# Small matmuls set one by one between long passes: scores, values and transposes of an attention and feed-forward kernel

## The chip, the cores and the metric

The kernel runs on one core of a Trainium2 chip. What is measured is the device time of one execution in microseconds (us). TensorE does the matmuls, ScalarE the tables and copies, VectorE elementwise work and sums, GpSimd (POOL) more elementwise work, and SyncE (SP) issues transfers.

## The reference

Two branches share one layer norm of `x` (4 batches of 1024 tokens, 512 wide), and both are added to it:

```python
xn = _layernorm(x)
x = x + attn(xn) + ffn(xn)
# attn: 8 heads, q and k of 32 per head, v of 64
h_in = _rmsnorm(x, norm1_w)
q, k, v = h_in @ wq, h_in @ wk, h_in @ wv          # by head
o_pre = h_in @ w_og
i_pre = soft_cap(h_in @ w_ig + b_ig); f_pre = soft_cap(h_in @ w_fg + b_fg)
Fcum = cumsum(log_sigmoid(f_pre))
Dmat = where(causal, Fcum[s] - Fcum[t] + i_pre[t], -inf); m = max(Dmat)
C = (q @ k.T / sqrt(32)) * exp(Dmat - m)
h = (C / maximum(abs(sum(C)), exp(-m))) @ v
h_out = sigmoid(o_pre) * rmsnorm_per_head(h)
x1 = x + h_out @ w_out
h2 = _rmsnorm(x1, norm2_w)
attn = x1 + silu(h2 @ w_gate) * (h2 @ w_up) @ w_down     # 2048 wide
# ffn: the same form, 1376 wide, its weights read from a table of 16 by indices
ffn = silu(x @ Wg.T) * (x @ Wu.T) @ Wd.T,  W = lut[idx]
```

## The kernel before, in words

**Blocks.** The work goes in eight blocks of 512 tokens, two per batch. Large matmuls work on operands split in a high and a low part and make three passes of 512 columns for each 128 of the inner dimension (high with high, low with high, high with low; `split`, L797): 12 passes for 512. A block of the attention branch has a **front** (`front`, L1073: gates, twelve projections `proj(n)`, L813, of 12 passes each, 0 to 3 for q and k, 4 to 7 for v, 8 to 11 for the output gate) and eight **units** (one per chunk of 128 tokens and group of four heads). A unit u is three pieces on TensorE: `unit_1` (four score matmuls, L879), `unit_2` (one matmul `kv`, L888, and four of the values, L891, each fp32 and so two instructions in the trace), `unit_3` (state, L899). Between them the other engines make exponentials, products and head sums.

**Tiles.** The feed-forward part of a block has 16 **tiles**, each `gate` and `up` (12 passes each) and `down` of the tile before (8 passes with `hidden_hi`, L1021, then 4 with `hidden_lo`, L1024). The tiles of one block run beside the units of the next: `tiles` (L1101) holds a table `fill` of what stands after `gate`, after `up` and after `down` of tile t. In tiles 0 to 7 these are `unit_1(t)`, `unit_2(t)` and `unit_3(t)`; then come `out_proj`, in tile 10 the transposes `h2_T` (L932), in tile 15, ahead of `down`, the sixteen transposes `x_T` (L943) of the next block's normed input, four banks of four. After the tiles follow `gates` of the next block (L1038), which needs `x_T` split in high and low parts by ScalarE (L1199) and VectorE (L1673), and the last `down`. In the front the transposes `q_k_T(i)` of q and k (L849) stand between whole projections, four for each chunk i of 128 tokens, all in the one bank `gate_bank`; ScalarE copies it twice (L1385, L1386) and VectorE subtracts for the low part (L1844). `gate_rows` (L1058) and `factors` (L1066) are small transposes for the gates.

**The first block.** It has no block before it, so its eight units run beside the projections of the second: for each u, `unit_1(u+1)`, nine passes of `proj(u-1)`, `unit_2(u)`, the last three passes, `unit_3(u)`. Then come `proj(6)`, `gate_rows`, `proj(7)`, `ho_T(3)` (transposes of the attention output, L844), `proj(8)`, four `out_proj`, `h2_T` with `proj(9)` and `proj(10)` between and after, `factors`, `proj(11)`, and the tiles.

**The end.** After the last attention block its 16 tiles run alone, and then the second branch: eight blocks of 11 tiles, with nothing between them. Its weights are decoded by `look` steps, beside the attention work, on ScalarE (L1274 to L1304) and VectorE.

**Order.** Every engine runs a program written out by hand, in order; the engines wait for each other by counters. Loads are issued by SP in its own written order. On ScalarE a tile is, among others, `hid(t-1)` (makes `hidden_hi`, L1212), the tanh of `gate` (L1207), exponentials, `h2_T` evacuations at t = 10, and the look-up steps; the low part of the hidden values comes from POOL (L2195). VectorE's order in the first block has `gate_factors` (L1820) between `x1_(0)` and `x1_(1)` (L1735), POOL's the four `x1_root` and `mlp_lo_` (L2180).

Of the kernel before, what the change touches and what calls it, by code (L numbers as in the profile page):

```python
# [5 lines left out]
P = 128  # L6
D = 512
KT = D // P
H = 8
DQ = 32  # L10
DV = 64
VS = DV + 1
# [138 lines left out]
def program(nc, x, w_attn, w_gates, norm1, b_gates, mh_w, norm2, w_mlp, lut, idx, out):  # L151
# [3 lines left out]
    with ctx:  # L155
# [636 lines left out]
        def _(pe):  # L792
# [11 lines left out]

            def pair(t, *ix):
                return (t[0][ix], t[1][ix])
# [6 lines left out]
            def proj(at, n, begin=0, end=3 * KT):  # L813
# [35 lines left out]
            def q_k_T(at, i):  # L849
                wait(pe, act_qk, at, i, "k")  # L850
                if i:
                    wait(pe, act_qkT, at, i - 1, "done")
                    if not here(at, FIRST):
                        wait(pe, vec_qkT, at, i - 1, "lo")
                else:
                    tiles_left(pe, MLP.gated, at)
                transposes(GB, [qn(at, i)[:, g * P:(g + 1) * P] for g in range(G)]
                           + [kn_(at)[:, i, g * P:(g + 1) * P] for g in range(G)], pe_qkT)

            def unit_1(at, u):  # L860
# [17 lines left out]
                for h in range(HG):  # L878
                    mm = pe.matmul(B[:, toks(h)], stack[0:3 * DQ, u % 2, 1, toks(h)], stack[0:3 * DQ, u % 2, 0, toks(h)],  # L879
                                   start=True, stop=True)  # L880
                mm.then_inc(pe_unit.sem, 1)

            def unit_2(at, u):
# [5 lines left out]
                for h in range(HG):  # L889
                    c = (j * H + g * HG + h) * VS  # L890
                    mm = pe.matmul(pick(at, u, A, ACC[0])[:, h * P:h * P + VS], pick(at, u, ct, ct2)[:, h, :], va_(at)[:, c:c + VS], start=True, stop=True)  # L891
                mm.then_inc(pe_unit.sem, 1)
# [39 lines left out]
            def h2_T(at, i):  # L932
                wait(pe, vec_h2, at, i)
                if here(at, FIRST):
                    wait(pe, vec_x1, at, i, "x1")
                elif i < 2:
                    wait(pe, vec_x1, at, i + 2, "x1")
                else:
                    wait(pe, vec_h2S, at, i - 2, "scaled")
# [3 lines left out]
            def x_T(at, i, src):  # L943
# [10 lines left out]
                elif here(at, FIRST):  # L954
                    if i >= 2:
                        wait(pe, vec_xT, at, i - 2, "lo")
# [1403 lines left out]
```

## Time and profile before

| | |
|---|---|
| median of 3 runs | 2401.63 us (2400.05 to 2402.75) |
| the profiled execution | 2400.62 us |
| its span in the trace | 2398.8 us |
| mean granted TensorE clock | 0.998 |
| TensorE busy | 2364.2 us, 99%, 11424 instructions |
| VectorE, ScalarE, POOL busy | 50%, 37%, 27% |

The span runs from the first instruction to the last in the trace; the execution's own time is 1.8 us longer. Busy time of TensorE counts a pass as it lies in the pipeline, so 99% says that something is nearly always in it, not that it runs at its peak. One row of the timeline is a group of like instructions: start, duration from the first start to the last end, engine, line, operation, output and inputs, count, and in brackets the idle time before it with what ended it.

### The profile page before, as it was taken

The page shows a single profiled execution, that of the slowest core. Times are in us where ns is not written, and L with a number is a line of the kernel's source. Part 1 is how long each engine was busy: PE and PEld are TensorE (multiplying, and loading weights), DVE is VectorE, ACT ScalarE, POOL GpSimd, SP SyncE. Part 2 cuts the span into 40 slices and gives each one's busy share as a digit, 9 for nine tenths or more (in the row PEclk, how much of TensorE's full clock was granted, in tenths as well). Part 3 has the DMA queues.
Part 4 walks back from the last instruction along what each step waited for, and adds up shares of the span by engine and source line. Part 5 has one row for each costly group of instructions (what it writes and reads, how often), then busy time and mean ns, then how long its engine had stood idle before and what let it go on. Part 6 is the DMA issues. An engine that isn't in the chain of part 4 may idle for free. (4 is left out here: it accounts for less than half of the span.)

```text
span 2398.8 us, 30880 instructions
## 1 busy us (share of the span) xinstructions
PE 2364.2 (99%) x11424; PEld 1937.2 (81%) x11424; DVE 1197.9 (50%) x2133; ACT 899.1 (37%) x1653; POOL 636.4 (27%) x494
## 2 busy tenths in 40 slices
PE   8899999999999999999999999999999999999999
PEld 6677888888888888888888888888888888888887
DVE  6776536665674674567467466642222222222222
ACT  6533244444445454445545453562111111111111
POOL 2356513223331321322232232322111111111111
PEclk9999999999999999999999999999999999999999
DMA  6277576576567558657755764766876876876865
GB/s 241 77 246 254 225 284 213 197 280 221 180 238 260 190 206 291 198 186 249 245 194 207 276 214 171 274 239 213 301 255 239 298 250 241 300 251 238 302 217 208
DMA packets 184035, 561.76 MB, mean 234 GB/s; under 512 B 17968, under 2 KB 75568, under 8 KB 148688
## 3 DMA queue, kind: packets, MB, share of 16 engines
q1 hardware_dynamic: 158400, 518.50, 61.9%
q10 hardware_dynamic: 25488, 41.30, 5.2%
q8 instruction: 92, 1.51, 0.3%
q14 instruction: 55, 0.45, 0.1%
HBM read 456.18 MB, written 102.50 MB: 233 GB/s over the span
## 5 line engine op out<-in xcount | busy, mean ns | idle before, releaser
L801 PE MATMUL gate_bank<-act_hi,gud 128*128 128x512 f32 x1728 | 573.5, 393 | 0.5 <-DVE th L1724 0.5
L801 PE MATMUL up_bank<-act_hi,gud 128*128 128x512 f32 x1728 | 572.8, 393 | 0.0
L2195 POOL TENSOR_TENSOR hidden_lo<-hm,hidden_hi 128x512 fp32r<-128x512 f32 x215 | 281.5, 1309 | 1035.0 <-ACT hidden_hi L1212 1035.0
L1021 PE MATMUL acc<-gud,hidden_hi 128*128 128x512 f32 x1720 | 433.5, 394 | 4.6 <-ACT hidden_hi L1212 4.6
L1724 DVE SCALAR_TENSOR_TENSOR th<-th,gate_bank 128x512 f32<-128x512 f32 x216 | 147.7, 684 | 510.4 <-ACT th L1207 510.2
L1212 ACT ACTIVATE hidden_hi<-hm 128x512 fp32r<-128x512 f32 x215 | 135.2, 629 | 673.5 <-PE acc L1024 673.1
L801 PEld LDWEIGHTS gate_bank<-act_hi,gud 128*128 128x128 f32 x1728 | 324.6, 188 | 69.5 <-issue 0.9
L801 PEld LDWEIGHTS up_bank<-act_hi,gud 128*128 128x128 f32 x1728 | 324.8, 188 | 66.2
L1021 PEld LDWEIGHTS acc<-gud,hidden_hi 128*128 128x128 f32 x1720 | 317.5, 188 | 70.8 <-issue 7.3
L801 PE MATMUL gate_bank<-act_lo,gud 128*128 128x512 f32 x864 | 337.0, 390 | 0.0
L801 PE MATMUL up_bank<-act_lo,gud 128*128 128x512 f32 x864 | 336.4, 389 | 0.0
L1207 ACT ACTIVATE th<-gate_bank 128x512 f32<-128x512 f32 x216 | 128.6, 595 | 388.3 <-PE gate_bank L801 388.3
L1730 DVE SCALAR_TENSOR_TENSOR hm<-th,up_bank 128x512 f32<-128x512 f32 x216 | 148.4, 687 | 242.9 <-PE up_bank L801 238.6
L1024 PE MATMUL acc<-gud,hidden_lo 128*128 128x512 f32 x860 | 229.9, 389 | 0.0
L1290 ACT ACTIVATE look_w<-look_w,lt,ld 128x512 f32<-128x512 int32 x280 | 216.1, 804 | 12.8 <-DVE look_w L1710 12.8
L1024 PEld LDWEIGHTS acc<-gud,hidden_lo 128*128 128x128 f32 x860 | 161.5, 188 | 33.6
L801 PEld LDWEIGHTS up_bank<-act_lo,gud 128*128 128x128 f32 x864 | 162.5, 188 | 32.1
L801 PEld LDWEIGHTS gate_bank<-act_lo,gud 128*128 128x128 f32 x864 | 162.4, 188 | 31.8
L1719 DVE COPY_PREDICATED look_w<-look_w 128x512 f32<-128x512 int32 x228 | 173.8, 810 | 11.6 <-ACT look_w L1280 7.6
L2204 POOL TENSOR_TENSOR mq<-mq,maskd 128x1024 f32<-128x1024 f32 x32 | 80.0, 2510 | 234.1 <-DMA mq<-max_rows 234.1
L2150 POOL TENSOR_TENSOR rh<-sm,half_pow 128x8 f32<-128x8 f32 x32 | 60.3, 1884 | 183.4 <-DVE sm L1934 183.4
L2186 POOL TENSOR_TENSOR look_w<-look_w 128x512 fp32r<-128x512 f32 x35 | 58.7, 1677 | 135.4 <-ACT look_w L1304 135.4
(324 smaller groups left out, 2835.5 us busy)
## 6 DMA issues: line engine op xcount, KB each, us to landing
gud<-mlp_parts SPq DMA_DIRECT2D x112, 1024.0 KB, 5.1
gud<-ghost_parts SPq DMA_DIRECT2D x88, 1024.0 KB, 5.2
gud<-mlp_parts SPq DMA_DIRECT2D x112, 512.0 KB, 3.9
gud<-ghost_parts SPq DMA_DIRECT2D x88, 512.0 KB, 4.1
stack<-qk_parts SPq DMA_DIRECT2D x336, 64.0 KB, 2.1
ghost_parts<-look_w SPq DMA_DIRECT2D x35, 512.0 KB, 3.4
mq<-max_rows ACTq DMA_DIRECT2D x32, 512.0 KB, 5.0
mlp_parts<-gud SPq DMA_DIRECT2D x16, 1024.0 KB, 4.7
```

What stands on the lines that cost most here:

```text
L801: mm = pe.matmul(dst, l[a], r[c], start=first and k == 0 and n == 0, stop=last and k == len(lhs) - 1 and n == 2)
L1021: pe.matmul(ACC[i][:], HH[0][:, toks(i)], W3[:, z, 2, n, :], start=t == 0 and n == 0, stop=False)
L1024: mm = pe.matmul(ACC[i][:], HH[1][:, toks(i)], W3[:, z, 2, 0, :], start=False, stop=t == last)
L1207: act.activation(th[:], GB[:], ACT.Tanh, scale=0.5).then_inc(of.tanh.sem, 1)
L1212: act.activation(HH[0][:], hm[:], ACT.Copy).then_inc(of.hid.sem, 1)
L1290: ins = act.activation(level_of(n, what), bit0(), ACT.Identity, bias=lt[:, 2 * what:2 * what + 1], scale=ld[:, what:what + 1])
L1719: dve.copy_predicated(level_of(n, lower), mask_of(n, k).bitcast(i32), level_of(n, upper)).then_inc(look_vec, 1)
L1724: dve.scalar_tensor_tensor(th[:], th[:], 1.0, GB[:], ALU.add, ALU.mult).then_inc(of.gated.sem, 1)
L1730: dve.scalar_tensor_tensor(hm[:], th[:], 0.5, UB[:], ALU.mult, ALU.mult).then_inc(of.hm.sem, 1)
L2150: pool.tensor_tensor(dst, src, half_pow[:, 0:n], ALU.pow).then_inc(stage.sem, 1)
L2195: pool.tensor_tensor(HH[1][:], hm[:], HH[0][:].bitcast(f32), ALU.subtract).then_inc(of.low.sem, 1)
L2204: pool.tensor_tensor(mq[:, j % 2, :, :], mq[:, j % 2, :, :], maskd[:].unsqueeze(1).to_broadcast([P, H, P]), ALU.add).then_inc(pool_mq.sem, 1)
```

## The change

Nothing is computed otherwise; TensorE's instructions stand in another order, and three other engines follow it.

- Scores stand after each of the first four passes of `up`, values (units 1 to 7) after the first four passes of `down`.
- In tile 10, `h2_T(0)` and `(1)` stand between the passes of `up`, `(2)` and `(3)` between those of `down`; in tile 15 `x_T` is spread in the same way.
- `q_k_T(i)` is spread over passes 2, 4, 6 and 8 of projections 2 to 5.
- In tile 10 ScalarE makes `hidden_hi` right after the `h2_T` evacuations, before its look-up steps, no longer at the start of tile 11.
- First block: projections split 6 and 6 about `unit_2`, `gates` of the second block after `unit_2(0)`, `proj(6)` in unit 7, one projection each before `h2_T(0)` and `h2_T(2)`. VectorE does the first of the gate factors (`inter`) earlier and the rest after `x1_(1)`; POOL does `x1_root(0)` before `mlp_lo_`.

```diff
@@ proj @@
+                    if chunk is not None and c in (1, 3, 5, 7):
+                        q_k_T(at, chunk, c // 2)
@@ score, values @@
+            def score(at, u, h):
+
+                if h == 0:
+                    unit_1(at, u)
+                mm = pe.matmul(B[:, toks(h)], stack[0:3 * DQ, u % 2, 1, toks(h)], stack[0:3 * DQ, u % 2, 0, toks(h)],
+                               start=True, stop=True)
+                if h == HG - 1:
+                    mm.then_inc(pe_unit.sem, 1)
...
+                if here(at, FIRST) or u == 0:
+                    for h in range(HG):
+                        values(at, u, h)
@@ up @@
-                split(UB[:], [(W3[:, z, 1, 0, toks(k)], W3[:, z, 1, 1, toks(k)]) for k in range(KT)],
-                      [pair(act, S_, k, S_) for k in range(KT)]).then_inc(of.up.sem, 1)
+                for p, mm in passes(UB[:], [(W3[:, z, 1, 0, toks(k)], W3[:, z, 1, 1, toks(k)]) for k in range(KT)],
+                                    [pair(act, S_, k, S_) for k in range(KT)]):
+                    if p == 3 * KT - 1:
+                        mm.then_inc(of.up.sem, 1)
+                    if stage and t < UNITS and p < HG:
+                        score(stage, t, p)
+                    if stage and t == 10 and p < 2 * KT:
+                        h2_T(stage, p // KT, p % KT)
+                    if stage and t == NM - 1 and p < 2 * KT:
+                        x_T(stage, p // KT, XN[1 - stage[1]], p % KT)
@@ down @@
+                        if stage and t + 1 < UNITS and i < HG // 2:
+                            values(stage, t + 1, 2 * i + n)
+                        if stage and t + 1 == 10:
+                            h2_T(stage, 2 + i // 2, i % 2 * 2 + n)
+                        if stage and t + 1 == NM - 1:
+                            x_T(stage, 2 + i // 2, XN[1 - stage[1]], i % 2 * 2 + n)
@@ front @@
-                q_k_T(at, 0)
-                proj(at, 2)
-                q_k_T(at, 1)
-                proj(at, 3)
+                proj(at, 2, chunk=0)
+                proj(at, 3, chunk=1)
                 gate_rows(at)
-                q_k_T(at, 2)
-                proj(at, 4)
-                q_k_T(at, 3)
-                for n in range(5, 9):
+                proj(at, 4, chunk=2)
+                proj(at, 5, chunk=3)
+                for n in range(6, 9):
@@ first block @@
-                if u == 0:
-                    gates(SECOND)
-                elif u < 7:
-                    proj(SECOND, u - 1, 0, 9)
+                if u:
+                    proj(SECOND, u - 1, 0, 6)
...
                 unit_2(FIRST, u)
+                if u == 0:
+                    gates(SECOND)
...
-                if 0 < u < 7:
-                    proj(SECOND, u - 1, 9)
+                if u:
+                    proj(SECOND, u - 1, 6)
...
-            proj(SECOND, 6)
             gate_rows(SECOND)
             proj(SECOND, 7)
             ho_T(FIRST, NB - 1)
             proj(SECOND, 8)
             for i in range(NB):
                 out_proj(FIRST, i)
+            proj(SECOND, 9)
             h2_T(FIRST, 0)
             h2_T(FIRST, 1)
-            proj(SECOND, 9)
+            proj(SECOND, 10)
             h2_T(FIRST, 2)
             h2_T(FIRST, 3)
-            proj(SECOND, 10)
@@ ScalarE, tiles @@
-                        hid(MLP, mb, t - 1)
+                        if not stage or t != 11:
+                            hid(MLP, mb, t - 1)
...
                     if stage and t == 10:
                         for i in range(NB):
                             h2_T(i)
+                        hid(MLP, mb, t)
@@ VectorE, first block @@
                 x1_(at, 0)
+                gate_inter(SECOND)
+                x1_(at, 1)
                 gate_factors(SECOND)
-                x1_(at, 1)
```

**TensorE, tile 1 of a steady block, from the end of `up`.** Before: `kv`, the four values (`va`), then `down`.

```order
L888 MATMUL bank_b<-kv,qT 128x260 [waits vec_unit]
L891 MATMUL bank_a<-va,ct 128x65 x4
L1021 MATMUL acc<-gud,hidden_hi 128x512 [waits act_hid,ld_dn0,vec_out]
L1021 MATMUL acc<-gud,hidden_hi 128x512 x7
L1024 MATMUL acc<-gud,hidden_lo 128x512 [waits pool_hid]
L1024 MATMUL acc<-gud,hidden_lo 128x512 x3
```

After the change, the same place to the end of the tile:

```order
L906 MATMUL bank_b<-kv,qT 128x260 [waits vec_unit]
L1065 MATMUL acc<-gud,hidden_hi 128x512 [waits act_hid,ld_dn0,vec_out]
L915 MATMUL bank_a<-va,ct 128x65
L1065 MATMUL acc<-gud,hidden_hi 128x512
L915 MATMUL bank_a<-va,ct 128x65
L1065 MATMUL acc<-gud,hidden_hi 128x512
L915 MATMUL bank_a<-va,ct 128x65
L1065 MATMUL acc<-gud,hidden_hi 128x512
L915 MATMUL bank_a<-va,ct 128x65
L1065 MATMUL acc<-gud,hidden_hi 128x512 x4
L1074 MATMUL acc<-gud,hidden_lo 128x512 [waits pool_hid]
L1074 MATMUL acc<-gud,hidden_lo 128x512 x3
```

The values of unit 1 left the stretch ahead of `down` and stand one by one behind its first four passes.

**TensorE, the end of a steady block.** `xn` are the rows that `x_T` transposes; before, from `x_T(2)` to `gates` (`gates_w`):

```order
L846 MATMUL gate_bank<-ident,xn 128x128 [waits vec_gate,vec_ln]
L846 MATMUL gate_bank<-ident,xn 128x128 x3
L846 MATMUL up_bank<-ident,xn 128x128 [waits vec_hm,vec_ln]
L846 MATMUL up_bank<-ident,xn 128x128 x3
L1021 MATMUL acc<-gud,hidden_hi 128x512 [waits act_hid,mlp_lo_dn]
L1021 MATMUL acc<-gud,hidden_hi 128x512 x7
L1024 MATMUL acc<-gud,hidden_lo 128x512 [waits pool_hid]
L1024 MATMUL acc<-gud,hidden_lo 128x512 x3
L1038 MATMUL up_bank<-act_hi,gates_w 32x512 [waits vec_hm,vec_xT]
L1038 MATMUL up_bank<-act_hi,gates_w 32x512 x3
L1042 MATMUL up_bank<-act_lo,gates_w 16x512 x4
```

After the change, from the last transpose of `x_T(2)` to `gates`:

```order
L994 MATMUL gate_bank<-ident,xn 128x128
L1065 MATMUL acc<-gud,hidden_hi 128x512
L994 MATMUL up_bank<-ident,xn 128x128 [waits vec_hm,vec_ln]
L1065 MATMUL acc<-gud,hidden_hi 128x512
L994 MATMUL up_bank<-ident,xn 128x128
L1065 MATMUL acc<-gud,hidden_hi 128x512
L994 MATMUL up_bank<-ident,xn 128x128
L1065 MATMUL acc<-gud,hidden_hi 128x512
L994 MATMUL up_bank<-ident,xn 128x128
L1074 MATMUL acc<-gud,hidden_lo 128x512 [waits pool_hid]
L1074 MATMUL acc<-gud,hidden_lo 128x512 x3
L1088 MATMUL up_bank<-act_hi,gates_w 32x512 [waits vec_hm,vec_xT]
L1088 MATMUL up_bank<-act_hi,gates_w 32x512 x3
```

The bank of `x_T(3)`, `up_bank`, is complete behind the eighth pass with `hidden_hi`, four passes ahead of `gates`, where it was twelve.

**TensorE, the front, chunk 0 and chunk 1 of `q_k_T`.** `vw` holds q and `kn` k. Before, chunk 0 with the projection's last passes ahead and its successor's first behind:

```order
L839 MATMUL bank_a<-qk_w_lo,act_hi 128x512
L839 MATMUL bank_a<-qk_w_hi,act_lo 128x512
L846 MATMUL gate_bank<-ident,vw 128x128 [waits vec_gate,act_qk]
L846 MATMUL gate_bank<-ident,vw 128x128
L846 MATMUL gate_bank<-ident,kn 128x128 x2
L839 MATMUL bank_b<-qk_w_hi,act_hi 128x512 [waits act_qk]
L839 MATMUL bank_b<-qk_w_lo,act_hi 128x512
```

After the change, the first ten passes of projection 3 with the transposes of chunk 1:

```order
L845 MATMUL bank_a<-qk_w_hi,act_hi 128x512 [waits act_qk]
L845 MATMUL bank_a<-qk_w_lo,act_hi 128x512
L869 MATMUL gate_bank<-ident,vw 128x128 [waits vec_qkT,act_qkT,act_qk]
L845 MATMUL bank_a<-qk_w_hi,act_lo 128x512
L845 MATMUL bank_a<-qk_w_hi,act_hi 128x512
L869 MATMUL gate_bank<-ident,vw 128x128
L845 MATMUL bank_a<-qk_w_lo,act_hi 128x512
L845 MATMUL bank_a<-qk_w_hi,act_lo 128x512
L869 MATMUL gate_bank<-ident,kn 128x128
L845 MATMUL bank_a<-qk_w_hi,act_hi 128x512
L845 MATMUL bank_a<-qk_w_lo,act_hi 128x512
L869 MATMUL gate_bank<-ident,kn 128x128
```

The chunk's four transposes stood together behind a whole projection; now each has two passes between it and the next, and the wait for the bank (`vec_qkT`, `act_qkT`) falls in the midst of a projection.

## Rows read from the trace of the kernel before

**Rows 1.** The page: the span, and the busy time of each engine.

```profile
span 2398.8 us, 30880 instructions
...
PE 2364.2 (99%) x11424; PEld 1937.2 (81%) x11424; DVE 1197.9 (50%) x2133; ACT 899.1 (37%) x1653; POOL 636.4 (27%) x494
```

**Rows 2.** TensorE's waits: waited for, us in total, times, longest us.

```profile
PE acc L1021 <- ACT hidden_hi L1212: 4.6, 6, 0.8
...
PE acc L846 <- DVE kn_first L1753: 1.8, 1, 1.8
```

**Rows 3.** Timeline, end of a steady block: start, us, engine, line, operation.

```profile
511.08 0.60 PE L846 MATMUL bank_b<-ident,xn 128*128 128x128 f32 x4
...
513.17 0.62 ACT L1199 ACTIVATE act_hi<-up_bank 128x512 fp32r<-128x512 f32 x1
...
514.15 0.68 DVE L1673 TENSOR_TENSOR act_lo<-up_bank,act_hi 128x512 fp32r<-128x512 f32 x1
...
514.66 1.07 PE L1024 MATMUL acc<-gud,hidden_lo 128*128 128x512 f32 x4
...
515.57 1.10 PE L1038 MATMUL up_bank<-act_hi,gates_w 128*32 128x512 f32 x4
```

**Rows 4.** Timeline, scores and values in a tile of a steady block.

```profile
404.99 0.56 PE L879 MATMUL bank_b<-stack 96*128 96x128 f32 x4
...
405.67 0.39 PE L801 MATMUL up_bank<-act_lo,gud 128*128 128x512 f32 x1
...
408.64 1.00 PE L891 MATMUL bank_a<-va,ct 128*128 128x65 f32 x8
...
411.37 1.07 PE L1024 MATMUL acc<-gud,hidden_lo 128*128 128x512 f32 x4
```

**Rows 5.** Timeline, front of a steady block, chunks 0 and 3 of `q_k_T`.

```profile
526.21 0.38 PE L846 MATMUL gate_bank<-ident,vw 128*128 128x128 f32 x2
...
526.88 0.40 PE L839 MATMUL bank_b<-qk_w_lo,act_hi 128*128 128x512 f32 x1
...
527.14 0.60 ACT L1385 ACTIVATE stack<-gate_bank 128x512 fp32r<-128x512 f32 x1
...
527.62 0.39 ACT L1386 ACTIVATE qT<-gate_bank 128x256 f32<-128x256 f32 x1
...
528.04 0.69 DVE L1844 TENSOR_TENSOR stack<-gate_bank,stack 128x512 fp32r<-128x512 f32 x1 [3.46 <-ACT qT L1386]
...
535.73 0.65 DVE L1844 TENSOR_TENSOR ct<-gate_bank,qbd 128x512 fp32r<-128x512 f32 x1
...
536.52 0.41 PE L846 MATMUL gate_bank<-ident,vw 128*128 128x128 f32 x2
```

**Rows 6.** Timeline, 0.08 us about the first score: matmul and weight load (PEld).

```profile
404.99 0.22 PE L879 MATMUL bank_b<-stack 96*128 96x128 f32 x1
404.99 0.19 PEld L879 LDWEIGHTS bank_b<-stack 96*128 96x128 f32 x1
```

**Rows 7.** Timeline, tile 11 of a steady block: `hidden_hi` and `down`.

```profile
477.59 0.61 ACT L1212 ACTIVATE hidden_hi<-hm 128x512 fp32r<-128x512 f32 x1
...
478.35 2.07 PE L1021 MATMUL acc<-gud,hidden_hi 128*128 128x512 f32 x8 [0.77 <-ACT hidden_hi L1212]
```

**Rows 8.** Timeline, first block from unit 7 to the first tile.

```profile
105.23 0.45 PE L899 MATMUL acc<-vw,kn_first 128*32 128x65 f32 x8 [2.75 <-DVE hr L1899]
...
109.31 0.68 DVE L1947 TENSOR_TENSOR act_lo<-up_bank,act_hi 128x512 fp32r<-128x512 f32 x1
...
111.40 0.60 PE L1058 MATMUL up_bank<-ident,gt 128*40 128x128 f32 x4
...
144.49 0.69 DVE L1769 TENSOR_TENSOR act_lo<-ct,act_hi 128x512 fp32r<-128x512 f32 x1
...
145.84 0.39 PE L801 MATMUL gate_bank<-act_hi,gud 128*128 128x512 f32 x1
```

**Rows 9.** Windows: stretch, us, busy of PE, PEld, DVE, ACT, POOL; PEclk, DMA share, GB/s.

```profile
104.00:111.10 7.10, 5.87 (x23) 4.73 (x24) 5.14 (x13) 0.60 (x1) 1.63 (x1) 0.52 0.51 159
```

More of the change, by code:

```diff
@@ L803, in split, with passes @@
                 return mm
+            def passes(dst, lhs, rhs):
+                for k, (l, r) in enumerate(zip(lhs, rhs)):
+                    for n, (a, c) in enumerate(((0, 0), (0, 1), (1, 0))):
+                        yield 3 * k + n, pe.matmul(dst, l[a], r[c], start=k == 0 and n == 0, stop=k == len(lhs) - 1 and n == 2)
             def pair(t, *ix):
@@ L811, in toks, with proj @@
                 return slice(i * P, (i + 1) * P)
-            def proj(at, n, begin=0, end=3 * KT):
+            def proj(at, n, begin=0, end=3 * KT, chunk=None):
                 kind, i = n // NB, n % NB
@@ L847, in transposes, with q_k_T @@
                 mm.then_inc(stage.sem, 1)
[L849 to L858, printed above, removed]
+            def q_k_T(at, i, s=None):
+                if not s:
+                    wait(pe, act_qk, at, i, "k")
+                    if i:
+                        wait(pe, act_qkT, at, i - 1, "done")
+                        if not here(at, FIRST):
+                            wait(pe, vec_qkT, at, i - 1, "lo")
+                    else:
+                        tiles_left(pe, MLP.gated, at)
+                for k in range(2 * G) if s is None else (s,):
+                    src = qn(at, i)[:, k * P:(k + 1) * P] if k < G else kn_(at)[:, i, (k - G) * P:(k - G + 1) * P]
+                    mm = pe.transpose(GB[:, k * P:(k + 1) * P], src, ident[:])
+                if s in (None, 2 * G - 1):
+                    mm.then_inc(pe_qkT.sem, 1)
             def unit_1(at, u):
@@ L930, in out_proj @@
                       [pair(WO, S_, k, S_) for k in range(KT)]).then_inc(pe_out.sem, 1)
[L932 to L939, printed above, removed]
-                f = (h2_rows0 if here(at, FIRST) else h2_rows)[i]
-                transposes(ACC[i] if here(at, FIRST) else AB[i % 2], [f[:, k * P:(k + 1) * P] for k in range(KT)], pe_h2T)
@@ new lines, in x_T @@
+            def x_T(at, i, src, s=None):
+                if not s:
+                    if here(at, PRE):
+                        if i % 2:
+                            pe.wait_ge(act_xn, i // 2 + 1)
+                        else:
+                            wait(pe, vec_ln, at, 0, f"xn{i // 2}")
+                    else:
+                        wait(pe, vec_ln, at, 0, f"xn{i}")
+                    if here(at, PRE):
+                        pass
+                    elif here(at, FIRST):
+                        if i >= 2:
+                            wait(pe, vec_xT, at, i - 2, "lo")
+                    elif i < 2:
+                        wait(pe, vec_h2S, at, i + 2, "scaled")
+                    else:
+                        wait(pe, MLP.gated if i == 2 else MLP.hm, previous(at), NM - 1)
+                for k in range(KT) if s is None else (s,):
+                    mm = pe.transpose(xt_bank(at, i)[:, k * P:(k + 1) * P], src[:, i, k * P:(k + 1) * P], ident[:])
+                if s in (None, KT - 1):
+                    mm.then_inc(pe_xT.sem, 1)
@@ L1862, in front @@
                     qkT_lo(at, 3)
+                gate_inter(at)
                 gate_factors(at)
```

73 lines of the change are left out of this document (34 added, 39 removed).

## The prediction

> **What bounds the kernel now.** I read the page first, for the shares, then the view of TensorE's waits, then TensorE's timeline tile by tile, and last the rows of ScalarE and VectorE around the places that the change touches. TensorE is busy 99% of a span of 2398.8 us [rows 1]; the profiled execution took 2400.6 us, 1.0 below the median of 2401.6, so what is summed against it is raised by 1.0 at the end. TensorE has one late partner in the steady blocks: six waits of 0.77 us for `hidden_hi`, 4.6 us in all; nearly all its other waits lie in the first block [rows 2]. So the time is TensorE's instruction stream plus a few waits, and the change must be priced by what a small matmul costs in its new place and by which waits it removes or makes.
>
> **What a small matmul costs.** A pass of 512 columns follows the last after 0.227 us (four passes from 514.66 to 515.57) [rows 3]. The four scores start at 404.99 and the second pass after them at 405.67: 0.68 less one pass is 0.45, 0.113 each. The eight instructions of the values (each fp32 matmul is two) start at 408.64; `hidden_lo` follows at 411.37 behind eight passes (1.82), which leaves 0.91, 0.114 each [rows 4]. The four transposes of a chunk take 526.88 - 526.21 - 0.227 = 0.443, 0.111 each [rows 5]; the sixteen of `x_T` take 514.66 - 511.08 - 1.82 = 1.76, 0.110 each [rows 3]. Groups of 4 and of 16 cost the same per member, so a group has no large cost of its own that scattering its members could save or multiply. The reason shows in the weight loads: the second score's load starts at 404.99, the moment the first score's matmul starts, not earlier under the pass before [rows 6]. One load runs ahead, never two. A score between two passes has its own load hidden, but the load of the pass behind it can only begin when the score does: the pass waits for it just as the next score did. I therefore price the interleaving at a few ns per new group (0.443 less four times 0.110 is 0.003). Per block the groups rise from 8 to 32 (scores), 7 to 28 (values), 2 to 16, 1 to 16 and 4 to 16 (transposes): from 22 to 108, 86 more, about 600 in seven blocks. **+1.8 us**; ends 0 and, at twice that and more, 5.
>
> The Trainium skill, page "TensorE: Matmul & The Clock Gate", section "Step-by-step: what each phase is for", says that TensorE pulls weight loads ahead of matmuls in flight when they target the background buffer. Taken freely, so that the next pass's load too is done before the small matmul ends, it would make this the large gain of the first rival; the loads of this trace show it one deep only, and the sum goes by the rows.
>
> **ScalarE's `hid` at t = 10.** In tile 11 `down` waits 0.77 us for `hidden_hi`, which ScalarE makes at 477.59, behind seven table look-up steps [rows 7]. The change makes it before those steps. The wait goes, with the 0.16 by which a shown matmul (0.39) outlasts the pass spacing: 0.93 in six blocks. The `h2` transposes now end later, and VectorE's and ScalarE's work behind them slips by about 1 us; what is late next is the tanh of tile 11, and if that runs out, `gate` of tile 12 waits a few tenths in its place, which the lower end takes in. **-5.6 us**; ends -6 and -2.
>
> **`x_T` at the end of a block.** Before, all sixteen transposes stand ahead of `down`, so twelve passes lie between the last of them and `gates` of the next block, which needs the VectorE remainder of `x_T(3)`. Now `x_T(3)` ends after the eighth pass of `down`: four passes (0.91) and its own 0.11 remain, 1.02. Needed are the transpose's end (about 0.27 after its start), ScalarE's copy 0.62, VectorE's subtract 0.68 [rows 3] and 0.11 of hand-overs, 1.68. TensorE stands about 0.65 at each of seven block ends (`gates` six times, the tail's first `gate` once); ScalarE's copy of `x_T(2)` is done by then and doesn't queue. **+4.6 us**; ends 0 and 7.
>
> **`q_k_T` in the projections.** All four chunks use one bank, `gate_bank`, and a chunk may only start when ScalarE has copied the one before twice (0.60 and 0.39, started 0.48 apart, 0.87 together) and VectorE has subtracted (0.69) [rows 5]. Before, a whole projection of twelve passes (2.72) lay between two chunks, and only the last waited: its first transpose stands at 536.52, the subtract ends at 536.38 [rows 5], and by the pass spacing it is about 0.3 late. Now a chunk's transposes stand after passes 2, 4, 6 and 8 of one projection, the next chunk's first after pass 2 of the next: six passes and 0.11, 1.47. Needed: 0.27 + 0.87 + 0.69 + 0.11 = 1.94. TensorE stands 0.47 from chunk 0 to 1 and from 2 to 3; from 1 to 2 `gate_rows` (0.44) covers most, but there ScalarE comes from `gate_logs`, which now starts later, so 0.1. That is 1.0 against 0.3 before, 0.7 in each of six fronts. **+4.2 us**; ends 0 and 12.
>
> **Edits at nothing.** Scores finish about 0.9 us later in `up`, values about 0.9 later in `down`; VectorE's product with the exponentials and its two head sums still come before `kv` and `unit_3` in a steady block, whose wait list is empty of them [rows 2]. If that cover went, `unit_3` would wait. `h2_T` in tile 10 keeps about the distance that its two banks had. No transfer is moved on SP's queue; the load of `stack` for unit u+2 waits for the scores of u, and has a whole tile.
>
> **The first block.** The projections are split six and six about `unit_2`, `gates` stands after `unit_2(0)`, and `proj(6)` moves into unit 7. `unit_3(7)` waited 2.75 us [rows 8] and now has six passes ahead. But the chain of VectorE sets these waits, and two things hold the gain. First, `gate_rows` needs `up_bank`, free once VectorE has done `act_lo` at 109.31 + 0.68, 4.76 us after `unit_3(7)` at 105.23 [rows 8]. `proj(6)` covered that; now TensorE stands there for about 4 us. If `unit_3(7)` comes 1.2 us earlier (between 0.3 and its 2.75), `gate_rows` starts at 108.8 in place of 111.40: 2.6 gained. That idle is longer than the 2.75 after which the granted clock fell to half, 0.52 over 104.0 to 111.1 [rows 9], a level of 1.2 for 2.4 GHz; here it would fall on `proj(7)`, whose twelve passes (2.7) would take up to twice as long; I let it take 0.8 back. 1.8 is left. Second, `proj(9)` fills the waits between `out_proj` and the `h2` transposes, 1.8 us for the longest [rows 2], but `gate(0)` can't start before VectorE's last `h2` remainder, 144.49 + 0.69, and starts at 145.84 now [rows 8]: 0.6 can be had, and up to 2.4 if moving `inter` ahead of `x1_(1)` shortens VectorE's chain. I take 1.5. **-3.3 us**; ends +1 and -6.
>
> **The sum.** 2400.6 + 1.8 - 5.6 + 4.6 + 4.2 - 3.3 = 2402.3 for an execution like the profiled one; 1.0 higher against the median: **2403**. About 0.2% (4.8 us) is what a measurement of this kernel can tell from no change: 2396.8 to 2406.4 is "same".
>
> **Rivals.**
> - *Two loads ahead.* If a small matmul between two passes costs its columns alone (128 columns, a quarter of the 0.227 of 512, 0.057 against 0.113), the 108 groups of a block save 0.056 each in seven blocks, 42 us: 2361. For it: nothing in this trace shows a lone small matmul. Against: [rows 6]. Chance 0.10.
> - *The new waits don't come.* If ScalarE and VectorE hand over faster than summed and both stalls (4.6 and 4.2) stay under a third, the sum is 2403 - 6, and with the first block at its better end 2394. For it: each is a difference of two close numbers. Against: both are built from shown durations. Chance 0.18.
> - *The chunk chain becomes the bound (slower).* In the front everything runs through ScalarE in order: chunk copies, `gate_logs` with its table loads, the evacuation of each projection. It decides once a chunk's copy starts more than 0.5 us after its transposes are done: then all three hand-overs cost about 1.0 instead of 0.47, 0.1 and 0.47, 2 us more in each of six fronts, with the last copies late for the exponentials behind them. With the first block's gain lost to the clock as well, 2403 + 9 = 2412 at its price and 2407 at half. For it: the same bank nearly waits already. Against: ScalarE is busy 37%. Chance 0.28.
> - My forecast, between 2397 and 2407: 0.44.
>
> The range reaches from the good end of the second rival to the full price of the third, 2393 to 2412, and leaves out the first rival and a little above. Faster by over 0.2%: 0.10 and most of 0.18, 0.26. Slower: 0.28 and a little of the forecast's own spread, 0.30. Same: 0.44.
>
> **What the profile after would show.** Right: a steady score or value still costs 0.11 with the pass behind it; the `hidden_hi` wait of tile 11 gone; a new wait of 0.6 to 0.7 us of `gates` (L1038 before) for `act_lo` seven times; waits of 0.4 to 0.5 of the chunk transposes for VectorE's subtract; about 4 us idle before `gate_rows` near 105 us, with half clock behind it. Wrong: a pass that follows a lone score after 0.06 instead of 0.11, or no waits for `act_lo` at the block ends.

## The result and the profile after

The changed kernel takes 2431.09 us in the median of four runs (2427.07 to 2434.49) against 2402.19: a ratio of 1.0121, 95% interval 1.0108 to 1.0133, 29 us slower. The forecast was 2403 with a range up to 2412, so the time lies outside it. The profiled execution took 2427.07 us, the shortest of the four, 26.4 above the one of before; what follows counts in that one, and the 4 us that the median has more come back below. Two executions in the experiments took 3952 and 4787 us, where all others of the same two kernels lie within 3 us of each other; they are left out of the ratios and move the medians by less than 0.2 us.

The page of the changed kernel, for [rows 1]:

```profile
span 2425.3 us, 30880 instructions
...
PE 2379.7 (98%) x11424; PEld 1926.6 (79%) x11424; DVE 1209.5 (50%) x2133; ACT 901.6 (37%) x1653; POOL 646.9 (27%) x494
```

TensorE's waits in the changed kernel (columns as in [rows 2]):

```profile
PE bank_b L854 <- DVE hn L1990: 7.0, 7, 1.4
PE up_bank L1108 <- issue: 3.8, 1, 3.8
PE up_bank L1088 <- DVE act_lo L1716: 2.9, 6, 0.5
...
PE gate_bank L801 <- DVE act_lo L1812: 2.6, 1, 2.6
PE bank_a L845 <- ACT va L1442: 2.5, 4, 0.7
PE gate_bank L869 <- DVE ct L1891: 2.5, 6, 0.5
PE gate_bank L869 <- DVE stack L1891: 2.3, 6, 0.4
...
PE gate_bank L801 <- DVE th L1767: 1.0, 4, 0.5
```

The six waits for `hidden_hi` are gone. In their place stand seven for `hn` (six of about 0.93 us and one of 1.4 in the second block), which the prediction had at nothing, six for `act_lo` at the block ends (and one more of 0.7 in the tail), twelve for the bank of the chunks, and four for `va`, which the prediction did not name.

To see where the 26.4 us lie, I took from each timeline the end of `hidden_lo` of every tile and compared the stretches from one to the next. The stretches of the fourth steady block (the front up to the end of tile 1), and the sum of the differences over the trace, which for the steady blocks is that of six:

| stretch | before | after | differences, all blocks |
|---|---|---|---|
| start to the second block's first tile | 163.74 | 165.93 | +2.2 |
| rest of the second block | 151.21 | 152.62 | +1.4 |
| front | 54.73 | 56.95 | +11.5 |
| the next six tiles | 10.49, 10.88 by turns | 10.57 to 10.99 | +2.6 |
| tile with `ho_T(3)` | 9.35 | 10.28 | +5.5 |
| tile 10 | 12.67 | 12.76 | +0.6 |
| tile 11 | 9.19 | 8.17 | -6.0 |
| tiles 12 and 13 | 8.16, 8.16 | 8.27, 8.58 | +3.1 |
| tile 15 and the block's last `down` | 9.93, 4.62 | 10.07, 5.25 | +5.0 |
| tail | | | +0.5 |

The 88 tiles of the second branch take 718.08 us in both.

The first row isn't the change's. TensorE reaches the first unit of the first block at 57.25 us in this profile and at 55.29 in the one of before, 1.96 later, and the experiments below show that this start varies by as much in either order of the first block. Counted from the first unit, the row is +0.2.

**A lone score.** The timeline of the changed kernel in `up`, matmuls and weight loads, for [rows 4] and [rows 6]:

```profile
399.17 0.39 PE L809 MATMUL up_bank<-act_hi,gud 128*128 128x512 f32 x1
...
399.39 0.22 PE L896 MATMUL bank_b<-stack 96*128 96x128 f32 x1
399.40 0.19 PEld L809 LDWEIGHTS up_bank<-act_lo,gud 128*128 128x128 f32 x1
399.45 0.45 PE L809 MATMUL up_bank<-act_lo,gud 128*128 128x512 f32 x1
399.51 0.19 PEld L896 LDWEIGHTS bank_b<-stack 96*128 96x128 f32 x1
399.74 0.22 PE L896 MATMUL bank_b<-stack 96*128 96x128 f32 x1
```

From score to score 0.35, of which a pass is 0.227: 0.12 for a lone score, about as in a group (0.113). The next pass's load starts at 399.40, when the score starts; the pass is issued 0.06 behind the score but lasts 0.45 in place of 0.39. One load ahead, no more: the first rival is out.

**The wait for `hn`.** In tile 8 of block (1,1) before (VectorE's product, the load and the transposes of `ho_T(3)`), and under it after:

```profile
644.37 0.69 DVE L1942 TENSOR_TENSOR hn<-hn,xn 128x512 f32<-128x512 f32 x1
...
645.11 0.42 PEld L846 LDWEIGHTS bank_b<-ident,hn 128*128 128x128 f32 x4 [0.45 <-DVE hn L1942]
645.11 0.65 PE L846 MATMUL bank_b<-ident,hn 128*128 128x128 f32 x4
```

```profile
654.43 0.69 DVE L1990 TENSOR_TENSOR hn<-hn,xn 128x512 f32<-128x512 f32 x1
...
655.17 0.66 PE L854 MATMUL bank_b<-ident,hn 128*128 128x128 f32 x4 [0.93 <-DVE hn L1990]
```

Before, `hn` ended at 645.06 and the transposes started at 645.11: there was no slack at all, and the load had already idled 0.45. TensorE's own waits didn't name it, but those of its weight loads did, a list that the prediction does not use (kernel before, engine PEld):

```profile
PEld bank_b L846 <- DVE hn L1942: 2.7, 6, 0.5
```

Six times, 0.45 each. The values of unit 7 end four passes (0.91) later now, and all of it arrives: 0.93.

**The front.** ScalarE and TensorE of the changed kernel, behind chunk 3 of block (2,0):

```profile
758.81 0.69 ACT L1442 ACTIVATE va<-bank_a,r 128x512 f32<-128x512 f32 x1 [1.98 <-issue]
758.83 1.29 ACTq L1394 DMA_DIRECT2D max_rows<-mx  x1
...
764.14 0.63 ACT L1390 ACTIVATE ex<-xn 8x512 f32<-8x512 f32 x1
765.32 0.82 ACTq L1402 DMA_DIRECT2D mq<-max_rows  x2
766.18 0.69 ACT L1442 ACTIVATE va<-bank_a,r 128x512 f32<-128x512 f32 x1 [1.42 <-DMA max_rows<-mx]
...
766.93 0.50 PE L845 MATMUL bank_a<-vo_w_hi,act_hi 128*128 128x512 f32 x1 [0.72 <-ACT va L1442]
```

and ScalarE of the kernel before in the same place of block (1,1):

```profile
540.12 0.47 ACTq L1353 DMA_DIRECT2D max_rows<-mx  x1
...
544.67 1.63 ACTq L1361 DMA_DIRECT2D mq<-max_rows  x2
...
546.62 0.63 ACT L1349 ACTIVATE ex<-xn 8x512 f32<-8x512 f32 x1
547.27 0.69 ACT L1401 ACTIVATE va<-bank_a,r 128x512 f32<-128x512 f32 x1
```

ScalarE stores the row maxima to memory (`max_rows`), does its exponentials, and reloads them with a wait for the store's landing; the evacuation of projection 7 (`va`) stands behind that wait. The chunks are spread, so chunk 3 ends later, its store later, and `max_rows` is issued 27.4 us after `gates` in place of 24.6. Before, the landing was hidden under the exponentials (547.27 follows 546.62 + 0.63 at once); now ScalarE idles 1.42 for it, and projection 9, which wants the bank, idles 0.72 behind that. In the fronts with spread chunks the reload goes out 4.5 to 8.0 us after the store, in this profile and those of the experiments.

That is one of the four waits for `va`. The other three (0.57, 0.58 and 0.63) stand earlier, at projection 7, for the evacuation of chunk 1 behind ScalarE's two stores of chunk 3 of q and k, as here in block (1,1):

```profile
548.88 1.31 ACTq L1436 DMA_DIRECT2D qk_parts<-hr  x1
...
550.24 0.69 ACT L1442 ACTIVATE va<-bank_a,r 128x512 f32<-128x512 f32 x1 [2.58 <-issue]
...
550.98 0.50 PE L845 MATMUL bank_a<-vo_w_hi,act_hi 128*128 128x512 f32 x1 [0.57 <-ACT va L1442]
```

In the three fronts that have this wait, ScalarE takes 1.31 to 1.37 us to issue the second store; in the other three 0.49 to 0.68, and 0.49 or 0.50 in all six of the kernel before. Why the issue takes longer in some of them is not shown.

**The first block.** TensorE and the windows of the changed kernel, for [rows 8] and [rows 9]:

```profile
106.84 0.32 PE L925 MATMUL acc<-vw,kn_first 128*32 128x65 f32 x8
...
111.56 1.01 PE L1108 MATMUL up_bank<-ident,gt 128*40 128x128 f32 x4 [3.82 <-issue]
...
146.26 0.47 PE L801 MATMUL gate_bank<-act_hi,gud 128*128 128x512 f32 x1 [2.55 <-DVE act_lo L1812]
```

```profile
110.00:116.80 6.80, 5.24 (x15) 4.11 (x16) 4.56 (x7) 0.59 (x1) 1.64 (x1) 0.50 0.20 57
147.40:150.90 3.50, 3.50 (x11) 2.70 (x10) 1.90 (x4) 3.40 (x7) 1.09 (x1) 0.52 0.93 262
```

`unit_3(7)` waits for nothing. It comes 1.6 us later than before on the trace's clock, but counted from the first unit it comes 0.4 earlier (49.58 for 49.94), where 1.2 was forecast. `gate_rows` idles 3.8, as forecast, and comes 1.8 earlier by the same count (54.31 for 56.11), where 2.6 was forecast. Behind the wait at `gate(0)` a second stretch of 3.4 us at half clock stands, which the kernel before doesn't have.

### The profile page after: what moved, and what is told of

Its sections match the earlier page's. It is cut to its first block and busy times, and to the rows that moved or that the text cites. A ratio compares the mean times of both kernels' runs of the same rounds, so it can differ in the third digit from the quotient of the medians.

```text
span 2425.3 us, 30880 instructions
## 1 busy us (share of the span) xinstructions
PE 2379.7 (98%) x11424; PEld 1926.6 (79%) x11424; DVE 1209.5 (50%) x2133; ACT 901.6 (37%) x1653; POOL 646.9 (27%) x494
## 5 line engine op out<-in xcount | busy, mean ns | idle before, releaser
L809 PE MATMUL up_bank<-act_hi,gud 128*128 128x512 f32 x1728 | 586.1, 398 | 0.0
L2244 POOL TENSOR_TENSOR hidden_lo<-hm,hidden_hi 128x512 fp32r<-128x512 f32 x215 | 296.8, 1380 | 1006.0 <-ACT hidden_hi L1253 1006.0
L1065 PE MATMUL acc<-gud,hidden_hi 128*128 128x512 f32 x1720 | 492.6, 411 | 0.0
L809 PE MATMUL up_bank<-act_lo,gud 128*128 128x512 f32 x864 | 347.1, 402 | 0.0
L1331 ACT ACTIVATE look_w<-look_w,lt,ld 128x512 f32<-128x512 int32 x280 | 216.1, 804 | 11.9 <-DVE look_w L1753 10.8
L1517 ACT ACTIVATE ex<-mq,rn 128x128 f32<-128x128 f32 x240 | 76.7, 391 | 67.0 <-DVE ct L1935 67.0
```

What stands on the lines that cost most here:

```text
L809: yield 3 * k + n, pe.matmul(dst, l[a], r[c], start=k == 0 and n == 0, stop=k == len(lhs) - 1 and n == 2)
L1065: pe.matmul(ACC[i][:], HH[0][:, toks(i)], W3[:, z, 2, n, :], start=t == 0 and n == 0, stop=False)
L1331: ins = act.activation(level_of(n, what), bit0(), ACT.Identity, bias=lt[:, 2 * what:2 * what + 1], scale=ld[:, what:what + 1])
L2244: pool.tensor_tensor(HH[1][:], hm[:], HH[0][:].bitcast(f32), ALU.subtract).then_inc(of.low.sem, 1)
```

## The experiments

The profiled times and stretches are compared with the change's own (2427.07), the medians with 2431.09.

### The values back in a group

```diff
-                if here(at, FIRST) or u == 0:
-                    for h in range(HG):
-                        values(at, u, h)
+                for h in range(HG):
+                    values(at, u, h)
...
-                        if stage and t + 1 < UNITS and i < HG // 2:
-                            values(stage, t + 1, 2 * i + n)
```

> The change with the four values of a unit back in one group behind kv, all else as changed. Theory (the last value of unit 7 ends four passes later, and ho_T(3), which had no slack before, waits that much for VectorE): the wait of ho_T(3) for hn in tile 8, 0.93 us in the steady blocks, falls under 0.1, the stretch of that tile goes from 10.3 back to about 9.4, seven times, 6.4 us with some 0.1 a block for the groups: the profiled time goes from 2427.1 to about 2420. Rival (it is the scores, which also end 0.9 us later, that make unit 7 late): the wait stays at 0.9 and only the 0.1 a block comes back, 2426.

Measured: 2422.96 (ratio to before 1.0085, 1.0068 to 1.0102), profiled 2422.17. The line for `hn` is absent from TensorE's waits, and the tile with `ho_T(3)` is back at 9.32 in the block of the table. The theory holds; the scores are late by as much in this run and nobody waits for them. The median falls by 8.1 us, the profile by 4.9 only: its fronts took 56.8 to 59.6, 6.1 us more in all than the change's, and hid part of the gain.

### q_k_T back between whole projections

```diff
-                proj(at, 2, chunk=0)
-                proj(at, 3, chunk=1)
+                q_k_T(at, 0)
+                proj(at, 2)
+                q_k_T(at, 1)
+                proj(at, 3)
                 gate_rows(at)
-                proj(at, 4, chunk=2)
-                proj(at, 5, chunk=3)
-                for n in range(6, 9):
+                q_k_T(at, 2)
+                proj(at, 4)
+                q_k_T(at, 3)
+                for n in range(5, 9):
```

> The change with the transposes q_k_T back between whole projections in the front, all else as changed. Theory A (spreading the chunks makes both the waits for the bank, 0.61 and 0.63 us of stretch a front, and, through ScalarE's order, the waits of projections 6 to 8 for va, 0.8 to 1.0 a front): the stretch of a front goes from 56.8 or more back to about 54.8, 2.1 in each of six fronts: 2427.1 becomes about 2414.5. Theory B (the va waits come from the later block end and stay): only the bank waits go, 1.1 a front: about 2420.5.

Measured: 2414.75 (1.0047, 1.0032 to 1.0062), profiled 2414.59. All six fronts take 54.84 to 54.89, and no wait for `va` is left: theory A. That its time came out to the microsecond is in part luck, for the fronts give back 10.8 us and another 1.7 comes from an earlier first unit (55.57 for 57.25). This is the largest part of the loss: 10.8 of the profiled 26.4, and 16 of the median's 29, for its four runs lie within 2.1 us where the change's lie within 7.4.

### The evacuations ahead of the transfers

```diff
                 qkT_(at, 3)
-                store_qk(at, 3)
                 v(at, 1)
+                store_qk(at, 3)
                 store_max(at)
                 v(at, 2)
                 exps(at)
+                if not here(at, FIRST):
+                    v(at, 3)
                 for j in range(2):
                     load_max(at, j)
...
-                v(at, 3)
+                    v(at, 3)
```

The old `v(at, 3)` stays for the first block alone. Two runs: the first with `va` of chunk 3 ahead of the loads alone, the second with `va` of chunk 1 ahead of the store too.

> The change with one edit on ScalarE: in the front it evacuates projection 7 (va of chunk 3) ahead of the two loads of max_rows, not behind. Theory (the load waits for the landing of the store of max_rows, which the spread chunks start about 3 us later, and the evacuation behind it then holds TensorE: 0.3 to 2.4 us, and differently from run to run): the waits for va after the factors matmuls vanish, the fronts' stretch is at most 56.9 each in place of up to 59.9 in the runs so far, and the runs' times lie closer together: profiled time 2425.5 to 2426.5, median about 2427 in place of 2431. Rival (the late part is VectorE's row work ahead of the exponentials, not the landing): the waits of that place stay, 2429 or more in the median.

> As the run with va of chunk 3 ahead of the loads, and in addition va of chunk 1 ahead of the store of chunk 3 of q and k. Theory (the 0.85 us waits of projection 7 for va come from that store, which waits for VectorE's subtract): all waits for va in the fronts vanish, what is left against before are the two waits for gate_bank (0.61, 0.63), the third's 0.18 and the groups, less the 0.35 of before: every front takes 55.9 to 56.1, and the profiled time is about 2421. Rival: the store, later by the evacuation, delays the load of stack or the row work, and the wait comes back at another place: 2425 or more.

Measured: 2425.13 (1.0099, 1.0085 to 1.0113; four runs within 1.5 us) and 2424.34 (1.0096, 1.0082 to 1.0109; profiled 2423.0). TensorE's waits for `va` with the first, and what replaces them with the second:

```profile
PE bank_a L845 <- ACT va L1442: 2.3, 4, 0.6
```

```profile
PE up_bank L1116 <- ACT ex L1390: 1.2, 2, 0.6
```

With the first, profiled at 2425.92, the waits behind the factors matmuls are gone (the four left are those of projection 7) and the four runs draw together, 6 us below the change's median: the landing of the `max_rows` store was on TensorE's path, and its varying length, with the half clock that follows the longer waits (below), accounts for most of the change's spread. The other kernels with that wait on the path spread by 3.7 to 5.8 us in four runs, those without it by 1.5 to 2.8. With the second, four fronts take 55.92 to 55.96, as expected; in the other two (56.6, 56.8) the factors matmuls wait for the exponentials instead, so the rival holds for a third of them. The time is nearer to the rival's (2425) than to the theory's (2421): the second edit gains 0.8 us in the median, not told apart from nothing.

### x_T back in a group

```diff
+                    if stage and t == NM - 1:
+                        for i in range(NB):
+                            x_T(at, i, XN[1 - at[1]])
                     if t:
                         down(MLP, mb, t - 1, NM - 1, stage)
```

with the two hunks of `x_T` in `up` and `down` taken out.

> The change with the sixteen transposes x_T of tile 15 back in one group ahead of down, all else as changed. Theory (gates waits 0.49 us for act_lo because x_T(3) ends only four passes ahead): that wait goes seven times (0.69 of stretch each in the trace, 0.93 in the tail), with 0.1 a block for 12 groups: 0.8 a block, 5.6 in all, 2427.1 becomes about 2421.5. Rival (the wait is taken up by the next one, the bank waits and va waits of the front, since ScalarE's work there starts from the same copy): less than 2 us, 2425.5.

Measured: 2424.87 (1.0094, 1.0079 to 1.0109), 6.2 below the change. In its profile, 2428.86 and the longest of its four, tile 15 and the last `down` are back at 9.93 and 4.62, while three fronts took 59.4 to 59.9, each with 3.4 us at half clock. The longest wait through the store (ScalarE, then TensorE):

```profile
347.35 0.69 ACT L1441 ACTIVATE va<-bank_a,r 128x512 f32<-128x512 f32 x1 [3.29 <-DMA max_rows<-mx]
...
348.09 0.50 PE L845 MATMUL bank_a<-vo_w_hi,act_hi 128*128 128x512 f32 x1 [2.23 <-ACT va L1441]
```

So the waits of `gates` go as the theory says, and the medians agree with it; in a single profile the spread of the landings can hide it.

### hidden_hi: early in the kernel before, late in the changed one

```diff
                     if t:
-                        hid(MLP, mb, t - 1)
+                        if not stage or t != 11:
+                            hid(MLP, mb, t - 1)
...
                         for i in range(NB):
                             h2_T(i)
+                        hid(MLP, mb, t)
```

is the edit to the kernel before; the second run takes it out of the changed one.

> The kernel before with one edit: in tile 10 ScalarE makes hidden_hi right after the h2_T evacuations, not after the look-up steps. Theory (the whole of the 0.77 wait was removable and the later transposes of h2 are what costs tiles 12 and 13 their 0.5 us in the changed kernel): tile 11 goes from 9.18 to 8.17 us in six blocks, tiles 12 and 13 stay at 8.16: 6.1 us less, 2396 against a before of 2402. Rival (hidden_hi taken early delays the tanh of the next tile behind the look-up steps, and this is what costs tiles 12 and 13): half of it is given back, 3 us less.

> The change with ScalarE's hidden_hi of tile 10 back behind the look-up steps, all else as changed. Same two theories as the run of before with this edit alone: theory (the spread h2_T costs tiles 12 and 13): tile 11 takes 1.0 us or more longer, as h2_T also ends later, and the 0.1 and 0.4 of tiles 12 and 13 stay: 2427.1 becomes 2433. Rival: tiles 12 and 13 fall to 8.16, so that only 0.5 a block is lost: 2430.

Measured: 2395.05 (0.9973, 0.9962 to 0.9984) and 2446.65 (1.0192, 1.0178 to 1.0206). In the kernel before, tile 11 falls by 1.02 and tiles 12 and 13 stay: the gain alone is 6.5 us in the median. In the changed kernel without it:

```profile
PE acc L1065 <- ACT hidden_hi L1253: 11.1, 6, 1.9
```

1.9 each, more than twice the wait of the kernel before, for the spread `h2_T` ends later; tile 11 takes 10.3 (11.8 once), and tiles 12 and 13 fall to 8.16 in four of the six blocks, as the rival had it; in the last block the two take 1.3 more, behind a wait of 1.0 for VectorE, and why is open. The 0.5 of the other blocks so needs both edits, the spread `h2_T` and `hidden_hi` early; as the next experiment and the kernel before with the one edit show too. Of the 19.2 us between the two profiles tile 11 has 14.2 and the fronts 9.1 (56.8 to 59.4); the rest goes the other way. Three of the fronts are near 59: there the wait for `va` behind the landing is 1.2 to 1.7 us, and the trace shows 3.4 us at half clock right behind it.

### h2_T back in groups

```diff
+                    fill[10, 0] = [(h2_T, 0), (h2_T, 1)]
+                    fill[10, 1] = [(h2_T, 2), (h2_T, 3)]
```

with its hunks in `up` and `down` taken out.

> The change with the transposes h2_T in tile 10 back in two groups ahead of up and ahead of down, all else as changed (hidden_hi early). Theory (the spread h2_T ends later, ScalarE comes late out of its evacuations, and the tanh and the product of tiles 11 and 12 are late for TensorE: +0.11 and +0.42 in tiles 12 and 13, which the run of before with hidden_hi early does not show): both tiles fall to 8.16, tile 10 loses its +0.09: 0.6 in six blocks, 3.7 us, 2427.1 becomes 2423.5, median 2427. Rival (what is late there is the look-up work, whose waits come from the longer front): the 0.5 stays, within 1 us of the change.

Measured: 2429.0 (1.0111, 1.0096 to 1.0127), 2.1 below the change and not told apart from it. The stretches are clear: tiles 10, 12 and 13 are at the 12.67 and 8.16 of before in every steady block, 0.6 less a block for the three together.

### The first block's old order

```diff
-                if u:
-                    proj(SECOND, u - 1, 0, 6)
+                if u == 0:
+                    gates(SECOND)
+                elif u < 7:
+                    proj(SECOND, u - 1, 0, 9)
```

and so on for the rest of the block, and for VectorE's and POOL's order.

> The change with the first block's order of before on TensorE, VectorE and POOL, the steady blocks as changed. The end of the first tile of the second block stands 2.2 us later with the change (165.9 against 163.7). Theory (the six-and-six split puts unit 7's values 3 us later, gate_rows idles 3.8 us and the half clock behind it and again at gate(0) takes the rest): that end goes back to 163.7 to 164.0 and the time from 2427.1 to about 2425. Rival (the first block costs nothing by itself, the 2.2 come from the gates and front in the changed form, which this run keeps): within 0.5 of 2427.

Measured: 2433.94 (1.0131, 1.0116 to 1.0146), 2.9 slower in the median, where I had expected 2 faster; the two sets of runs overlap, and the profile's fronts are 6.4 us longer than the change's. The theory falls, and with it the comparison that it rested on: the first unit starts anywhere from 55.3 to 57.5 us in these profiles, which changes the second block's start by 2 us whatever the order. Counted from the first unit, `gate(0)` stands 90.4 to 90.55 us behind it in three of the four profiles with the old order (this run and the kernel before among them) and 89.4 in the fourth, and 87.3 to 89.0 in the ten profiles with the new order: the new order gains 1.6 in the mean, and 3.4 us at half clock behind the wait at `gate(0)`, in five of the ten, take 1.7 of that back. The fourth old one and the two lowest of the new (87.3, 87.7) are those in which the half clock near `unit_3(7)` or `gate_rows` lasts 3.4 us and not 6.8.

### Parts of the change put together

All three stand on the kernel before, with `hidden_hi` early; beside it the first has the first block's new order, the second the scores spread, the third both.

```diff
+                    if stage and t < UNITS and p < HG:
+                        score(stage, t, p)
```

> The kernel before with two parts of the change: hidden_hi early in tile 10, and the first block's new order on TensorE, VectorE and POOL; nothing spread. Theory (in the profiles the new order brings gate(0) 1.5 to 1.7 us earlier counted from the first unit, but the 2.5 us wait ahead of it is followed by 3.4 us at half clock, which takes 1.7 back in the runs where it falls there): 2394 to 2395, not to be told from the run with hid early alone (2395.05). Rival (the half clock doesn't follow, as in two of the profiles): 2393.4, ratio to that run 0.9993.

> The kernel before with hidden_hi early and the scores alone spread between the first passes of up in the steady blocks. Theory (a lone score costs 0.117 with the pass behind it, against 0.1125 in a group of four, and nothing waits for the later last score): 0.02 a unit, 56 units, 1 us: 2396. Rival A (a lone small matmul costs its columns alone): 32 x 7 x 0.056 = 12.5 us less, 2382.5. Rival B (the last score, 0.9 us later, makes the exponential product and with it kv or ho_T(3) late): 0.3 to 0.9 in seven blocks, 2398 to 2402.

> The kernel before with three parts of the change: hidden_hi early, the first block's new order, the scores spread; everything else grouped. Theory (in the second block the spread scores took away two waits of unit_3 of 0.7 us each, and in the steady blocks they cost 0.18 each; the first block's order is worth 1.5 and pays part of it to the half clock): the sum is nothing that can be told from the runs with fewer parts, 2393.5 to 2395. Rival (the gains add up, since they lie in different blocks): 2392.5 or less.

Measured: 2394.56 (0.9967, 0.9955 to 0.9979), 2394.85 (0.9971, 0.996 to 0.9982) and 2395.29 (0.9968, 0.9956 to 0.9981), all one with 2395.05. In the second, a steady block takes 0.1 to 0.3 more than with `hidden_hi` early alone, 0.16 in the middle, 5 ns for each of 32 scores, and two waits of `unit_3` in the second block, 0.7 each, are gone. Rival A, a lone matmul at its columns alone, would have been 12.5 us faster. The gains don't add up to anything that can be told. Four kernels here are 0.3% faster than the kernel before, and the smallest edit, `hidden_hi` early alone, is as good as any.

## Why the prediction was wrong

The forecast for an execution like the profiled one was 2402.3, and it took 2427.07. In the terms of the table, what was found is 4.0 for the groups outside the front, -2.9 for `hidden_hi`, 4.7 for the wait at the block ends and the tail, 11.5 for the fronts, 6.9 for `hn` (its tile and the rest of the second block), and 2.2 up to the second block's first tile.

- **Small matmuls between passes, +1.8: the size.** Rightly a few ns each, 9 in place of 3: the unit tiles, tile 10, tile 15 and the chunks sum to some 0.8 us a block for 86 groups, 5 in all.
- **`hid`, -5.6: right**, and -6.5 alone. The lower end (tiles 12 and 13 give some back) came too, 3.1 us, and needs the spread `h2_T` beside the early `hidden_hi`.
- **`x_T`, +4.6: right.** The wait was forecast at 0.65 and is 0.49, of stretch 0.63; the last `down` of six blocks and the tail together are 4.7 longer. (The groups in tile 15, 0.14 a block, are counted above.)
- **`q_k_T`, +4.2: mechanism right, cut short.** The waits for the bank were forecast at 0.47 twice and are 0.38 and 0.39 (0.61 and 0.63 of stretch, as the passes restart), 6.4 us with the third's 0.18 and less the 0.35 of before. The step that failed is that it followed the bank only. The third rival named ScalarE's order in the front but looked at chunk copies; what was late were the evacuations behind the stores and the landing. Together the fronts are 11.5 longer in the profile, and grouping the chunks gives back about 16 in the median.
- **"Edits at nothing": the step that failed outright.** "Values about 0.9 later in `down`" was right, and "still come before `kv` and `unit_3`" too; I didn't ask who else waits for unit 7. `ho_T(3)` had 0.05 us left. It now waits 7.0 us, the second block included.
- **The first block, -3.3: right in kind, too large.** The idle of 3.8 at `gate_rows` and the half clock there came. Counted from the first unit, `unit_3(7)` comes 0.4 earlier in place of 1.2 (0.4 to 1.0 in the ten profiles; six passes of `proj(6)` now stand ahead of its own values, which may take the rest), `gate_rows` 1.8 in place of 2.6, and `gate(0)` 1.55; then the wait of 2.55 for VectorE ahead of it has half clock behind, which the forecast left out, and in this profile nothing is left (+0.2). The 2.0 by which the first unit itself starts later is chance.
- **The rivals.** The first is out: a lone score costs 0.12. The second is out: both new waits came, at 0.49 and 0.38. The third is the nearest, since ScalarE's order in the front decides, but its price is misadded: 2 us in each of six fronts and the lost 3.3 are 15, which makes 2418 and not the 2412 that sets the upper end of the range. The time lies above that too.

The range was too narrow for that slip and for a deeper reason: each end was set by the waits I had found, none by those I hadn't looked for.

## What to carry to other kernels

A step delayed by a known time is an edit at nothing only when every consumer's slack is read, and slack is read between the end of the producer and the start of the consumer, not from TensorE's list of waits, where a consumer without a wait can be one without slack (here the weight loads' list had it). When an evacuation stands behind a transfer's wait in an engine's order, everything that moves the transfer moves the evacuation, so put the work that another engine needs ahead of the wait. And where a small matmul costs the same in a group and alone, spreading has nothing to give and moves every result later.

## What the runs showed of the hardware

A wait for the landing of a small store that ended up on the path went with runs of one kernel that differ by 7.4 us (2427.07 to 2434.49); with what stood behind it out of the way, four runs lay within 1.5.

ScalarE's issue of the second store of chunk 3 took 0.49 to 0.9 us in 25 of the 48 profiled fronts with spread chunks and 1.2 to 1.4 in the other 23, and where it did, the evacuation behind it in ScalarE's order came late and projection 7 waited 0.5 to 0.7, unless the evacuation had been put ahead. In the kernel before and with the chunks grouped it took 0.49 or 0.50 in all twelve.

TensorE's clock fell to half (1.2 of 2.4 GHz) for 3.4 or 6.8 us about its longer waits: about the 3.8 us at `gate_rows` in all ten profiles that have it, about the 2.55 at `gate(0)` in five of the ten, and in the profiles of five experiments behind single waits of 1.2 to 2.2 us in the steady blocks, ten times in all. Three waits of 1.9 to 2.2 us for `va`, and five of the six of about 1.9 for `hidden_hi`, were not followed by it. A wait of 2 us can so cost nearly 4, or only itself.
